# Layer 2 of a gated cross-attention stack: batch-wise normalising, rounding on ScalarE, root epsilons on GpSimd, output projection ahead of the down product

## What is computed

```python
x = x + tanh(g_xattn[2]) * _L2_xattn_ref(_layernorm(x), ctx, mask, ...)
x = x + tanh(g_ffn[2])   * _L2_ffn_ref(_layernorm(x), w_gate, w_up, w_down)

def _L2_xattn_ref(...):                      # 16 heads of 16
    scores = clip(q k^T / 4, -50, 50)        # masked, clipped again
    probs = softmax(scores)
    ctx = probs @ v
    delta = rs * (ctx @ Wo.T + bo)
    return (delta - mean) / sqrt(var + 1e-5) * ln_gamma + ln_beta

def _L2_ffn_ref(...):                        # inner width 832
    bitlinear(x, w) = act_quant(x) @ weight_quant(w).T
    act_quant(x) = clip(round(x * s), -128, 127) / s,  s = 127 / max|x|
    return bitlinear(silu(bitlinear(x, w_gate)) * bitlinear(x, w_up), w_down)
```

## Time and profile before

| | |
|---|---|
| median of 3 runs | 1953.11 us (1948.66 to 1958.79) |
| the profiled execution, its own time | 1949.41 us |
| its span from first to last instruction | 1948.1 us |
| mean granted TensorE clock | 0.955 of full speed |
| busy share of the span: PE, DVE, ACT, POOL | 87%, 68%, 49%, 41% |
| chain that ended last, by engine | PE 51%, DVE 24%, ACT 8%, issue 8% |
| where layer 2's loop lies | about 1034 to 1265 us of the span |

### The profile page before, as it was taken

One profiled execution on the slowest core, in us unless ns is written; L12 is line 12 of the kernel. 1 busy time (PEld: TensorE's weight loads), 2 busy tenths in 40 slices (PEclk: granted clock), 3 DMA queues, 4 the chain that ended last, 5 costly groups with the idle time before them and its releaser, 6 DMA issues.

```text
span 1948.1 us, 35947 instructions
## 1 busy us (share of the span) xinstructions
PE 1702.4 (87%) x12191; PEld 1178.0 (60%) x12221; DVE 1327.5 (68%) x4195; ACT 945.2 (49%) x2227; POOL 789.6 (41%) x957
## 2 busy tenths in 40 slices
PE   6999988979897988989896787788999999987898
PEld 2444444646666777777684555456777777765445
DVE  7888874523466887887747888864667677667446
ACT  2767673213323777777544555334444444443352
POOL 3333321266654656664525454220143433343340
PEclk7999999989997999999898999799999999989898
DMA  4454422048843333443213543019010000031857
GB/s 110 103 124 104 97 54 90 23 157 304 287 138 84 85 88 84 95 84 68 74 37 102 154 120 82 17 37 322 1 36 19 33 10 1 13 98 37 240 192 307
DMA packets 180437, 200.41 MB, mean 103 GB/s; under 512 B 86500, under 2 KB 150129, under 8 KB 176928
## 3 DMA queue, kind: packets, MB, share of 16 engines
q1 hardware_dynamic: 164224, 156.32, 29.4%
q0 software_dynamic: 15168, 41.54, 6.2%
q10 hardware_dynamic: 864, 0.26, 0.1%
HBM read 131.88 MB, written 75.44 MB: 106 GB/s over the span
## 4 chain that ended last, share of the span: by engine, by line
PE 51%; DVE 24%; ACT 8%; issue 8%; POOL 4%; DMA 4%; SPq 1%; another core or an unknown queue 0%; DVEq 0%; ACTq 0%; POOLq 0%
PE psum L1058 4%; PE psum L3474 3%; PE psum L3400 3%; DVE sbuf L539 3%; PE psum L389 3%; PE psum L3449 2%; PE psum L352 2%; PE psum L3467 2%; PE psum L1337 2%; ACT sbuf L3837 2%; PE psum L2286 2%; PE psum L1070 2%; PE psum L1356 1%; PE psum L1702 1%; PE psum L4057 1%
## 5 line engine op out<-in xcount | busy, mean ns | idle before, releaser
L539 DVE TENSOR_REDUCE sbuf<-psum 128x2 f32<-128x512 f32 x256 | 164.5, 684 | 35.3 <-PE psum L352 34.2
L190 POOL TENSOR_TENSOR sbuf<-sbuf 128x1 f32<-128x1 f32 x128 | 73.2, 574 | 276.5 <-DVE sbuf L182 276.4
L2021 ACT ACTIVATE sbuf<-psum 128x512 f32<-128x512 f32 x256 | 137.8, 592 | 69.6 <-PE psum L1772 68.4
L3837 ACT ACTIVATE sbuf<-psum,sbuf 128x128 f32<-128x128 f32 x256 | 113.6, 455 | 89.8 <-DVE sbuf L3649 89.5
L678 ACT ACTIVATE sbuf<-psum 128x1024 f32<-128x1024 f32 x128 | 131.1, 1025 | 47.5 <-PE psum L374 43.1
L3929 POOL DMA_INDIRECT l_slot_inputs<-sbuf x96 | 97.0, 1011 | 102.0 <-DVE sbuf L3720 76.7
L3474 PE MATMUL psum<-sbuf 128*128 128x256 f32 x512 | 124.2, 386 | 4.9 <-DVE sbuf L3667 4.9
L352 PE MATMUL psum<-sbuf 112*128 112x256 bf16 x512 | 104.2, 288 | 16.3 <-DVE sbuf L539 11.2
L3400 PE MATMUL psum<-sbuf 128*128 128x256 f32 x512 | 117.0, 382 | 0.8 <-ACT sbuf L3801 0.8
L1897 DVE CUSTOM_DVE_ANT_0 sbuf<-psum,sbuf 128x128 f32<-128x128 f32 x512 | 112.6, 285 | 0.3 <-PE psum L1751 0.3
L3400 PEld LDWEIGHTS psum<-sbuf 128*128 128x128 f32 x512 | 97.1, 192 | 20.6 <-issue 8.6
(11 more groups left out here) (436 smaller groups left out, 4474.0 us busy)
## 6 DMA issues: line engine op xcount, KB each, us to landing
l_pair_outputs<-sbuf SPq DMA_DIRECT2D x24, 512.0 KB, 7.1
sbuf<-in_l_gu_pairs SPq DMA_DIRECT2D x32, 384.0 KB, 8.1
sbuf<-l_pair_outputs SPq DMA_DIRECT2D x16, 768.0 KB, 15.9
sbuf<-l_q_parts SPq DMA_DIRECT2D x16, 384.0 KB
l_q_parts<-sbuf SPq DMA_DIRECT2D x64, 96.0 KB, 2.2
sbuf<-l_q_parts SPq DMA_DIRECT2D x32, 192.0 KB
l_k_parts<-sbuf SPq DMA_DIRECT2D x64, 96.0 KB, 2.1
sbuf<-l_k_parts SPq DMA_DIRECT2D x32, 192.0 KB
```

The lines of the kernel that those rows point to most:

```text
L539: dve.tensor_reduce(top3[:, 2 * hp:2 * hp + 2, c], score_bank[v % 2].rearrange("p (j t) -> p j t", j=2), AXX, ALU.max, negate=True).then_i ...
L2021: act.activation(e_t[i % 4][:, h * BANK:(h + 1) * BANK], turn_bank[:, h * BANK:(h + 1) * BANK], ACT.Exp).then_inc(*exped.up())
L3837: last = act.activation(e_t[u % 3][:, j * P:(j + 1) * P], score_bank[:, j * P:(j + 1) * P], ACT.Exp, bias=mt[:, j:j + 1], scale=rq[:, lo + ...
```

## The change

1. Weighing and normalising go by batch. `pe_weigh(b)` does both units into all 512 columns of `av_bank` and `dve_normalise(b)` transposes, inverts, multiplies and transposes both at once. Rows of Wo and of the value bias are put in another order on the host side of the layout (`by_group`) to fit.
2. The rounding of h leaves `dve_ffn_gate` for a new `act_round_h` on ScalarE, with a new constant `plus_round`.
3. The epsilon additions of `ln_stats` and `dve_delta_stats` leave VectorE; GpSimd adds epsilon ahead of each root (`ln_root_of_variance`, `pool_delta_root`).
4. The orders of all engines' programs change: on TensorE `pe_project_out(i - 1)` comes between the scores and `pe_down(f)`, and `pe_turn_hq(f)` behind the weighing; on VectorE the gate comes behind the FFN statistics and the statistics ahead; on ScalarE rounding and `act_keep_hq` come behind `act_less_mean` and `act_mid`; on GpSimd the roots and the norm of a pair come earlier and its two betas an iteration later, behind `pool_add_out`.

```diff
+def ln_root_of_variance(m, n, var_ready, eps_added, rstd_ready, ring):
+    pool, s = m.nc.gpsimd, ring[n % len(ring)]
+    pool.wait_ge(*var_ready.at(n + 1))
+    pool.tensor_scalar(s[:, 8:9], s[:, 7:8], EPS_LN, None, ALU.add).then_inc(*eps_added.up())
+    pool.wait_ge(*eps_added.now())
+    pool.tensor_tensor(s[:, 8:9], s[:, 8:9], m.half_neg, ALU.pow).then_inc(*rstd_ready.up())
...
+    def pe_weigh(b):
+        pe.wait_ge(*clipped.at(2 * b + 2))
+        pe.wait_ge(*v_ready.at(b + 1))
+        if b:
             pe.wait_ge(*x_mid.at(b))
...
     def pe_project_out(b):
-        pe.wait_ge(*normed.at(2 * b + 2))
-        pe.wait_ge(*av_read.at(min(2 * b + 3, 2 * NB)))
+        pe.wait_ge(*normed.at(b + 1))
...
     def pe_program():
         for i in range(NB):
-            if y >= 0:
-                pe_project_out(y)
             if paired and i % 2 == 0:
                 pe_keys(i // 2 + 2)
             if paired and i % 2 == 1:
                 pe_queries(i // 2 + 2)
             pe_scores(2 * i + 1)
             if paired and i % 2 == 0:
                 pe_turn_x(i // 2 + 2)
-            if f >= 0:
-                pe_turn_hq(f)
             if i + 2 < NB:
                 pe_values(i + 2)
             if i:
-                pe_weigh(2 * i - 1)
+                pe_weigh(i - 1)
             if f >= 0:
-                pe_down(f)
-            pe_weigh(2 * i)
+                pe_turn_hq(f)
             if y >= 0:
                 pe_turn_xq(y)
             if i + 1 < NB:
                 pe_scores(2 * i + 2)
+            if i:
+                pe_project_out(i - 1)
+            if f >= 0:
+                pe_down(f)
             if y >= 0:
                 pe_up(y)
...
     def dve_program():
         for i in range(NB):
-            if i % 2 == 1:
-                dve_clip(2 * i)
+            if y >= 0:
+                dve_delta_stats(y)
+            dve_clip(2 * i)
+            if y >= 0:
+                dve_add_attention(y)
+                dve_ffn_stats(y)
+            if i % 2 == 1 and i // 2 + 3 < NPAIR:
+                dve_norm_stats(i // 2 + 3)
             if f >= 0:
                 dve_ffn_gate(f)
             if y >= 0:
-                dve_delta_stats(y)
-            if i % 2 == 0:
-                dve_clip(2 * i)
-            if y >= 0:
-                dve_add_attention(y)
-                dve_ffn_stats(y)
+                dve_ffn_quantise(y)
             if i:
-                dve_normalise(2 * i - 1)
-            if y >= 0:
-                dve_ffn_quantise(y)
+                dve_normalise(i - 1)
             dve_clip(2 * i + 1)
-            dve_normalise(2 * i)
-            if i % 2 == 1 and i // 2 + 3 < NPAIR:
-                dve_norm_stats(i // 2 + 3)
...
-        dve_ffn_gate(NB - 3)
         dve_delta_stats(NB - 2)
         ahead.dve_keep_queries(0, 0)
         dve_add_attention(NB - 2)
         dve_ffn_stats(NB - 2)
-        dve_normalise(2 * NB - 1)
+        dve_ffn_gate(NB - 3)
         dve_ffn_quantise(NB - 2)
+        dve_normalise(NB - 1)
         dve_ffn_add(NB - 3)
...
+    def act_round_h(f):
+        act.wait_ge(*h_scaled.at(f + 1))
+        act.activation(h_t[f % 2], h_t[f % 2], ACT.Identity, bias=plus_round, scale=s_t[f % 3][:, 9:10]).then_inc(*h_round.up())
...
     def act_program():
             if i % 2 == 0 and j < 2 * NPAIR:
                 act_keep_x(i // 2 + 2)
-            if f >= 0:
-                act_keep_hq(f)
             if i + 2 < NB:
                 act_values(i + 2)
             if y >= 0:
                 act_less_mean(y)
             if j < 2 * NPAIR:
                 act_mid(j)
             if f >= 0:
-                act_scale_out(f)
+                act_round_h(f)
+                act_keep_hq(f)
             if y >= 0:
                 act_keep_xq(y)
             if i + 1 < NB:
                 act_exp(2 * i + 2)
+            if f >= 0:
+                act_scale_out(f)
             if y >= 0:
                 act_tanh(y)
...
     def pool_program():
-            f, y, j, pair = i - 3, i - 2, made_in(i), i // 2 + 3
+            f, y, j, pair = i - 3, i - 2, made_in(i), (i - 1) // 2 + 3
             if y >= 0:
                 pool_delta_root(y)
             if j < 2 * NPAIR:
                 pool_rest(j)
+            if y >= 0:
+                ln_root_of_variance(m, y, f_var, eps_added, f_rstd, ffn_stats)
+            if i % 2 == 1 and pair < NPAIR:
+                pool_roots(pair)
+                pool_norm(pair)
             if f >= 0:
                 pool_out_scale(f)
             if y >= 0:
-                ln_root(m, y, f_var, f_rstd, ffn_stats)
+                pool_scales(y)
             if j < 2 * NPAIR:
                 pool_lo(j)
-            if y >= 0:
-                pool_scales(y)
             if f >= 0:
                 pool_add_out(f)
-            if i % 2 == 1 and pair < NPAIR:
-                pool_roots(pair)
-                pool_norm(pair)
+            if i % 2 == 0 and i and pair < NPAIR:
                 for n in range(PAIR * pair, PAIR * pair + PAIR):
                     pool_add_beta(n)
```

## The result

| | before | after |
|---|---|---|
| median, us | 1950.88 (1939.39 to 1958.79, 4 runs) | 1981.78 (1978.81 to 1986.86, 4 runs) |
| ratio to before | | 1.0176, 95% interval 1.0145 to 1.0207 |
| span of the profiled execution | 1948.1 | 1980.9 |
| mean granted TensorE clock | 0.955 | 0.943 |
| PE, DVE, ACT, POOL busy | 87%, 68%, 49%, 41% | 87%, 66%, 49%, 40% |

The change costs 31 us by the medians and 32.8 us by the spans. The forecast was slower by 15.7.

What follows compares the result with a forecast made beforehand. VectorE was taken to bound the loop; the new order's chains would replace it. Even +5.6, odd +7.1, i = 3 and 11 +2, late 0, start −3, end +4: +15.7 us, so 1969 (own range 1958 to 1980; overall 1945 to 1985).

Steps and rivals of the forecast that it cites:

- start: Up to the first up product, two batch normalisings replace five half batches on VectorE: −3 us (ends 0 and −5).
- i = 3: Iteration 3, walked as an odd iteration without `pool_add_out` or two statistics: about 14.8 us for 13.8, +1.
- i = 11: Iteration 11, walked as an odd iteration without `pool_add_out` or two statistics: about 14.8 us for 13.8, +1.
- i = 12 to 15: Late iterations without keys, queries or betas: walk 13.5 us, 1 to 1.5 added for TensorE's clock; called equal, ±4 in all.
- end: Behind the loop, batch 13's gate moves behind layer 3's copy of queries, delaying batch 14's up product: +4 us (0 to +6).
- Which waits: Quantise waits 1.5 us or more for less-mean (even), second delta step for GpSimd (odd); VectorE busy near 10 us.
- rival (a): VectorE stays the bound, so its relief of 2.2 us over 13 iterations counts: 28.6 us faster, 1924; chance 0.12.
- The even walk: Even iterations 4 to 10: one chain from up through keys, ScalarE, quantise, normalise, projection, down: 15.25 us against 13.86.
- The odd walk: Odd iterations 5, 7, 9: chain through GpSimd's add, betas and root, then statistics, gate, quantise, normalise: 16.1 us against 13.74.
- rival (c): TensorE's clock falls after odd-iteration idling, 1 to 3 us more in up to nine iterations: 1981 to 1994; chance 0.08.
- The batch multiply: In VectorE's normalise, two multiplies become one of 256 columns, taken at 0.45 us (0.4 to 1.1).
- The test by the gate's starts: In the profile after, distances between starts of the gate's first instruction should be near 15 and 16 us in turn.

Runs made afterwards that it cites:

- the filled kernel: The changed kernel with 14 (even iterations with keys: 5) extra unused bf16 matmuls on TensorE ahead of the transposes of h: 1970.51 us, ratio 1.0079 to before.
- fillers in both kernels: Extra unused TensorE matmuls ahead of the transposes of h, in the changed kernel (ratio 1.0079) and in the kernel before (3, then 12 from i = 12; 0.9973).
- the later low part: The changed kernel with GpSimd's subtraction for the lowest part (`pool_lo`) one iteration later, behind the next delta root: 1980.04 us, ratio 1.0133 to before.
- GpSimd's order: The changed kernel with `pool_add_out` and the two betas moved behind the next delta root on GpSimd: 1965.94 us, ratio 1.0054 to before.
- the end as before: The changed kernel with batch 13's gate again ahead of the delta statistics and layer 3's query copy, `pe_weigh` and `act_less_mean` likewise: 1980.06 us, ratio 1.0132 to before.

## Why the forecast was right in sign and wrong in size

Layer 2, term by term (forecast, then measured between before and after):

| term | forecast | measured |
|---|---|---|
| start | −3 | −3.1 (41.94 − 45.00) |
| i = 3 | +1 | +1.2 |
| i = 4 to 10 | +12.7 | +22.2 (120.37 − 98.16) |
| i = 11 | +1 | +4.0 |
| i = 12 to 15 | 0 ± 4 | +3.3 (62.3 − 59.0) |
| end | +4 (0 to +6) | +10.5 (44.01 − 33.52) |
| sum | +15.7 | +38.1, less 5.3 outside the layer |

*Which waits.* Right. The quantisation waits 3.55 us for less-mean in even iterations, the second delta step 2.64 for GpSimd in odd ones, VectorE has 10.5 to 11.8 us of work left and is not the bound. The wait named for rival (a), the relief, is far from zero. What I left out is that the GpSimd wait is there in even iterations too (2.47), because `pool_add_out` alone stands ahead of the root; it is hidden by the ScalarE chain there.

*The even walk* (forecast 15.25). In i = 6, cut the same way: up to bias 5.03 (forecast 3.44), bias to less-mean 4.59 (4.63), less-mean with its hand-off 0.53 (0.56), quantise 1.49 (1.45), normalise to the projection 2.64 (1.9), projection 1.59 (1.59), down and scale-out up to the next up product 1.75 (1.63 with hand-offs). Sum 17.62. Every step but two is within 0.15 us. The two are up and keys at the low clock, +1.6, and the multiply with its hand-off, +0.7.

*The odd walk* (16.1). In i = 7: up to the second delta step 2.72 (2.89), add and statistics 2.14 (2.56), gate 3.87 (4.0), quantise 1.71 (1.45), normalise 1.85 (1.9), then **0.66 that the walk doesn't have**, projection 1.68 (1.59), down 1.14 (1.06), scale-out 0.62 (0.47). Sum 16.39. The 0.66 is TensorE late for the projection: transposes of h 1.76, of x 0.63 and scores 1.06, all low. In i = 5 and 9 the low level lasted through projection and down (2.08, 1.81) and gave 18.24 and 17.99.

*The failed step* is thus that the sum walked i = 4 to 10 with TensorE's steps at the high clock and put the low level there at nothing, by the sentence in rival (c) that "most of the slow work lies beside normalise", and the chance of 0.08 that hung on it. The result, 1981.8, is that rival's time, 13 us above the forecast; its mechanism is right, but that the number falls into its range is partly luck, since the end and the multiply below belong to that distance too. The part of the clock is 8.3 us of the seven middle iterations by the filled kernel; that kernel also brings i = 12 to 15 from 62.3 to 54.3 us, 8.0 more. The comparison "the new order idles TensorE as long before the same transposes" was made with a late iteration (3.00 us) and doesn't hold in the middle: there the old order idled at most 1.27 us, with a mean clock of 0.98 over the seven iterations; after, the idle of 3.61 us comes in each odd one, and TensorE's own steps stand in the chain behind it. An odd iteration at the low level was longer than its filled counterpart by 0.6 to 2.2 us, so the price of 1 to 3 us was about right; that it would be rare was not. With fillers in both kernels the change costs 1.0079 / 0.9973 = 1.0106, about 21 us: that is nearer to the 15.7 of a walk at the high clock, and the clock is the other 13 or so of the 34 that 1.0176 makes.

*The batch multiply* was taken at 0.45 and took 1.07 in even iterations. The kernel with the later low part put 0.6 us on it per even iteration, 2.5 in four. That was in the bounds (0.4 to 1.1), but the row that it was nearest to was not the fast one: GpSimd's work was known to fall there. Clock 8.3 and multiply 2.5 close the seven iterations: 120.4 − 10.8 = 109.6, against 109.3 walked (4 × 15.25 + 3 × 16.1). The rest of the +9.5 error is the other way: before took 98.2 by up products, while the two stretches at 13.86 and 13.74 would make 96.7.

By the Trainium skill ("SBUF — State Buffer", Who interferes with whom) a VectorE instruction with two SBUF inputs contends with a GpSimd instruction that reads SBUF, and the shared pair of ports is an exclusive lock. The two rows agree, 1.07 beside L3187 and 0.43 without it, and the later low part shows it by experiment.

*i = 11* was forecast as an odd walk without the statistics ahead, 14.8, and took 17.30. Of the 2.5 above it some 2.2 are projection and down at the low level (2.08 and 1.81 us, with the bias row ahead of them) and 0.6 the multiply, which met the low part here too (1.04), other steps being 0.3 shorter; GpSimd's order alone brings it to 14.10 at a granted clock of 1.00, and the fillers alone to 16.40 at 0.90. The other 0.5 of the +4.0 is the old i = 11, which was 13.27 and not 13.8.

*The late iterations*: 13.31 us at a clock of 1.00 in the filled kernel against a walk of 13.5; 16.24 and 16.52 at granted clocks of 0.72 and 0.60 in the kernel after. Within ±4.

*The end*: the place was right, the gate behind layer 3's copy; the size was 6.5 us short. 1.5 of that is a slip in adding: 1272 and the terms given make 1282.5, not 1281. Another 1.0 was taken off for layer 3's products, which filled nothing. 2.1 is the copy, which ended 12.6 us after the up product of batch 13 instead of 10.5, since the sixteen products of queries that it waits for ran at the low level (5.70 us instead of 3.69). Turning h (1.75) and layer 3's keys cost some 1.2 more than forecast, and the last step 0.7. With the end as before 8.5 of the 10.5 us go.

*The start*: −3.1 meets the forecast of −3, but that is not shown to be its mechanism. The three profiles with the start of the kernel after have 41.94, 42.71 and 43.43 us to the first up product, the two with that of the kernel before 45.00 and 43.29.

*The even sum* of the forecast makes 15.30 with five hand-offs of 0.05, not 15.25; the odd one has 0.2 for the same five. Neither matters.

*The test by the gate's starts* ("near 15 and 16 in turn") was badly made. They came 19.84 and then 14.16 us apart (1122.71, 1142.55, 1156.71), since the gate stands at another place of the chain in even and odd iterations; the up product, which ends both, is the mark that works.

Left open: 5.3 us of the layer's 38.1 are missing in the span, and of the 8.5 that the old end saves in the layer 5.2 are seen there. What lies ahead of and behind the layer differs by such amounts between executions, and no run here separates it.

## What to carry to other kernels

When work is taken off the fullest engine of an in-order pipeline, walk the chain that ends at each product instead of counting load: here 1.5 us less work on VectorE went together with 3.2 us more per iteration, and moving three calls, 2 us of work, from ahead of the root on GpSimd gave back half of the layer's loss. Price TensorE's steps on such a chain at both clock levels wherever the new order leaves it idle ahead of them, 3.6 us here; a wait on another engine can cost twice, once by itself and once by the clock that falls in it. When two repairs are each tried alone, see the granted clock in both before adding their gains. An operation moved to another engine takes that engine's queue with it: the rounding took VectorE 0.76 us, and with it as the fourth in ScalarE's queue (and the epsilons on GpSimd) an iteration of the old order was some 3 us longer.

## What the runs showed of the hardware

- A ScalarE activation of 832 columns from SBUF to SBUF, with bias and scale read from columns, took 1078 ns; the tanh of the same width out of PSUM took 947.
- A GpSimd addition on 128x1 took 220 ns (L197); I had taken 335 from the earlier trace rows.
- Work that nothing needs made the kernel faster: 14 products in an idle gap, 2.64 us of TensorE, and the time of the kernel after fell from 1981.8 to 1970.5. In the kernel before, with 3 and 12 of them, it was worth 0.3% (ratio 0.9973).
- The same gap on TensorE at the same place of one kernel was followed by different levels: 1.98 us ahead of the values by low and by high weighing (1.76 and 1.08), 3.61 us ahead of the transposes of h by low and by high ones (1.76 and 0.98). The gap alone doesn't tell it; what a chain costs has to be priced at both levels.
- With the gap ahead of the transposes of h shortened from 3.61 to 1.77 us, by GpSimd's order and with no product added, the odd iterations had a granted clock of 1.00 instead of 0.81 to 0.90.
